# Graph attention on one core: the softmax sums in quarters of columns spread over a group, two accumulators for GpSimd, the residuals in other groups, the MLP weights cast in eight parts

## Chip, cores and metric

One core of a Trainium2 chip. The metric is the device time of one execution in microseconds (us); less is better. Engines: PE (TensorE), DVE (VectorE), ACT (ScalarE), POOL (GpSimd) and SP (SyncE, which here issues most DMAs). PE's weight loads have a row of their own in the profile, PEld.

## What is computed

A layer of graph attention over 2048 nodes with D = 256, 8 heads of 32 and a hidden width of 1024, all in float32:

```
h   = relu(layernorm(x))
hs  = layer_norm(h) * ln1_scale + ln1_bias          (sources)
ht  = layer_norm(h_target) * ln1_scale + ln1_bias   (targets)
q, k, v = ht @ Wq + bq, hs @ Wk + bk, hs @ Wv + bv  (q divided by sqrt(32))
probs = softmax(where(adj != 0, q k^T, -1e30))      (per head, 2048 x 2048)
y   = layer_norm(ht + (probs v) @ Wo + bo) * ln2_scale + ln2_bias
out = x + y + gelu(y @ W1) @ W2
```

The softmax takes no maximum: exponentials are used as they are, their sums are kept, and the context is divided by the sums later. (A slower path for very large values follows at the end and does not run on these inputs.)

## The kernel before

It is written by hand: each engine has its own program, and semaphores tie them together, so the order on an engine is the order of its code.

**Stages.** Layer norms, transposes and the projections of keys, values and queries come first (to about 66 us). Then the attention (to about 375 us), then the output products, the second layer norm and the MLP for four chunks of 512 targets.

**The attention loop** has 128 tiles. The targets are cut into 4 chunks `c` of 512 columns, the heads into 2 groups `g` of 4, the sources into 16 tiles `i` of 128. A tile is k = 32c + 16g + i, and G = 2c + g (0 to 7) counts the groups of 16 tiles. A tile holds two pairs of heads, u = 2k and 2k + 1, each a block of 128 x 1024 in a ring `probs` of 12 pairs, so 6 tiles. Per tile:

- PE, `scores` (L1387 to L1408): three times four products (high and low parts of keys and queries) of 512 columns into PSUM `slot` (three of them for pairs). It waits until DVE has emptied what the slots held.
- DVE, `mask` (L1017 to L1033): for each pair one instruction takes the minimum of scores and mask into `probs`.
- ACT, `exponentials` (L750): one exponential for each pair, in place.
- PE, `weigh` (L1410 to L1427): values times probabilities, four products of 512 columns side by side into `acc[:, 0]`. It waits for both exponentials of the tile.
- The sums of the probabilities over the 16 tiles. For the tiles in `ADDED` (L50) POOL adds them up into `added_up` (`add_up`, L535), two instructions per tile. For those in `TAKEN` PE multiplies them with ones into `acc[:, 1]` (`sum_weights`, L1429), one half of 256 columns in the tile's own iteration and one in the next. `close` (L1445) multiplies POOL's total with ones at i = 1 of the next group, and ACT copies the sums out (`evacuate_sums`, behind exponential u = 5 of the next group).

A float32 product is two passes on PE, so the profile counts four products as x8. PE runs two tiles ahead with the scores:

```
for k in range(NT):
    if k + 2 < NT:
        scores(k + 2)
    if k == NT - 2:
        attend(0)
    weigh(k)
    if k and (k - 1) % ST in TAKEN:
        sum_weights(k - 1, 1)
    if k % ST in TAKEN:
        sum_weights(k, 0)
    if k % ST == 1 and k > ST:
        close(k // ST - 1)
```

DVE masks a pair only when the ring's pair from six tiles back is done with: it waits for PE (`used`) and, for tiles in `ADDED`, for POOL (`added`).

**Around the loop.** At each chunk's end SP stores the sums, loads them packed, DVE inverts them (`invert`, at u % 64 = 14 of the next chunk, L1014), SP stores and spreads the inverses (`spread_inverse`, L387), and POOL multiplies the context with them (`divide`). In the last chunk SP issues the DMAs of W1 and W2 (L450, L451) just behind `spread_inverse(2)`; they go into the space of a mask that is no longer used (`w1_raw`, `w2_raw`, views of `maskT`). ACT casts W1 whole behind exponential 220 and W2 whole behind exponential 238 (`split_weights`, L768). POOL takes the difference w1_lo (L588) between the last chunk's two groups, DVE w2_lo (L1137) behind the loop. POOL also prepares the residual in `htn` (`make_residual`, L557), two instructions for each chunk.

**Behind the loop** PE does `attend(2)`, `turn_y(0)` (transposes, after DVE's layer norm of chunk 0), `attend(1)` and the first MLP products (`widen`). ACT loads the gelu table behind the last copy of the sums.

Of the kernel before, what the change touches and what calls it, by code (L numbers as in the profile page):

```python
# [32 lines left out]
def graph_attention(nc, x, adj, nodemask, h_target, ln1_scale, ln1_bias, Wq, bq, Wk, bk, Wv, bv, Wo, bo,  # L33
# [16 lines left out]
    ADDED = [0, 1, 3, 5, 7, 9, 11, 13]  # L50
    TAKEN = [i for i in range(ST) if i not in ADDED]
    OPS = (len(ADDED) - 1) * PAIRS

# [22 lines left out]
    with ExitStack() as ctx:  # L76
# [156 lines left out]
        ht_kept = sem("ht_kept")  # L233
        q_kept = sem("q_kept")
# [15 lines left out]
        used = sem("used")  # L250
# [80 lines left out]

        def packed(saved, c):
            return saved[:, cols_of(c)].rearrange("h (a b) -> h a b", b=PACK)
# [25 lines left out]
        SLOW_MIX = 8 + 3 * NEWTON + 5  # L359
        UG = PAIRS * ST  # L360
# [3 lines left out]
        def _(sp):  # L364
# [72 lines left out]
            for c in range(NCH):  # L437
# [22 lines left out]
            sp.wait_ge(used, NT)  # L460
# [50 lines left out]
        def _(pool):  # L511
# [23 lines left out]
            def add_up(c, g, i, pair):  # L535
                k = (c * GROUPS + g) * ST + i

                def at(tile):
                    return probs[:, ((k - i + tile) * PAIRS + pair) % RING]
                pool.wait_ge(exped, k * PAIRS + pair + 1)  # L540
                if i == ADDED[1]:
                    if k >= ST:
                        pool.wait_ge(closed, c * GROUPS + g)
                    nc.gpsimd.tensor_tensor(added_up[:, pair], at(ADDED[0]), at(i), ALU.add).then_inc(added, 1)  # L544
                else:
                    pool.wait_ge(added, added_through(k, pair) - PAIRS)
                    nc.gpsimd.tensor_tensor(added_up[:, pair], added_up[:, pair], at(i), ALU.add).then_inc(added, 1)  # L547
# [9 lines left out]
            def make_residual(c, step):  # L557
                h = htn[:, rows_of(c), :]
                if step == 0:
                    if c == 0:  # L560
                        pool.wait_ge(rest_made, 2)
                        pool.wait_ge(ht_kept, 16)
                    nc.gpsimd.tensor_tensor(h, h, gamma1_row[:, None, :].to_broadcast(wide), ALU.mult
# [6 lines left out]
            for c in range(NCH):  # L570
                for g in range(GROUPS):
                    for i in ADDED[1:]:
# [9 lines left out]
                    if c < LAST:  # L582
                        make_residual(c, g)
                    elif g == 0:
                        divide(c - 1, 0)
                        divide(c - 1, 1)
                        pool.wait_ge(w1_hi_made, 1)
                        nc.gpsimd.tensor_tensor(w1_lo[:], w1_raw, w1_hi[:].bitcast(F32), ALU.subtract  # L588
                                                ).then_inc(w1_lo_made, 1)
# [16 lines left out]
        def _(act):  # L606
# [161 lines left out]
            def split_weights(step):  # L768
                if step == 0:
# [3 lines left out]
                    nc.scalar.copy(w1_hi[:], w1_raw).then_inc(w1_hi_made, 1)  # L773
                else:
# [888 lines left out]
```

## Time and profile before

| | |
|---|---|
| median of three runs | 495.03 us (492.99, 495.03, 495.15) |
| profiled execution | 494.16 us, span 492.5 us |
| busy PE / DVE / ACT / POOL | 473.9 / 419.1 / 377.1 / 305.4 us |
| mean granted TensorE clock | 0.995 of full speed |
| DMA traffic | 46.92 MB, mean 95 GB/s |

The span runs from the first to the last instruction. Rows below are from this one execution. In a timeline, instructions of a kind that follow one another are merged into a row: start, length of the whole run, engine, line, operation, output and inputs, count, and, in brackets, the idle time just before it with what ended it. PE's products overlap one another in such rows, so PE's pace is read from starts. A clock of 1.00 is 2.4 GHz, 0.50 is 1.2 GHz.

### The profile page before, as it was taken

The numbers are of one execution on the slowest core, as the hardware profiler recorded it, in microseconds if no ns is written. First come the engines' busy times: TensorE is split into PE (matmuls) and PEld (weight loads), VectorE is DVE, ScalarE is ACT, GpSimd is POOL, SyncE is SP. The second block draws the span as 40 slices with busy tenths as digits, with TensorE's granted clock in tenths as the row PEclk, the third lists the DMA queues.
The fourth block names the chain that finished last, engine by engine and source line by source line (L and its number), as shares of the span: only waits on it lengthen the run. The fifth ranks groups of instructions, "written<-read, shape, count | busy, mean of one in ns | idle before, by whom it ended". The sixth has DMA issues, their size and how long they took to land.

```text
span 492.5 us, 10622 instructions
## 1 busy us (share of the span) xinstructions
PE 473.9 (96%) x4366; PEld 244.3 (50%) x4366; DVE 419.1 (85%) x631; ACT 377.1 (77%) x456; POOL 305.4 (62%) x152
## 2 busy tenths in 40 slices
PE   3999979999999999999999999999999999999995
PEld 1567523433333333333333333343434888888884
DVE  6889479999999999999999999999997977666343
ACT  4987968998998898998898998999995570727150
POOL 1000019996998999999999998999998300000000
PEclk9999989999999999999999999999999999999999
DMA  8997789723543674222772400070000100202021
GB/s 232 266 219 124 186 249 402 236 44 63 200 74 44 67 171 79 44 46 46 82 179 50 83 2 3 12 207 1 2 2 1 46 28 17 87 1 85 1 85 45
DMA packets 53774, 46.92 MB, mean 95 GB/s; under 512 B 35486, under 2 KB 46652, under 8 KB 53212
## 3 DMA queue, kind: packets, MB, share of 16 engines
q1 hardware_dynamic: 51216, 37.30, 28.3%
q0 software_dynamic: 2480, 8.92, 10.7%
q8 instruction: 35, 0.57, 0.5%
q14 instruction: 15, 0.12, 0.1%
q10 hardware_dynamic: 28, 0.01, 0.0%
HBM read 31.93 MB, written 14.81 MB: 95 GB/s over the span
## 4 chain that ended last, share of the span: by engine, by line
PE 61%; DVE 14%; issue 13%; ACT 5%; POOL 5%; DMA 1%; DVEq 0%; POOLq 0%
PE acc L1421 14%; PE slot L1406 13%; DVE probs L1032 10%; PE acc L1439 6%; PE slot L1521 3%; PE slot L1520 3%; PE slot L1519 3%; POOL added_up L547 3%; PE acc L1557 2%; PE acc L1558 2%; PE acc L1556 2%; PE slot L1472 2%; PE slot L1308 2%; DVE stats L852 1%; PE slot L1328 1%
## 5 line engine op out<-in xcount | busy, mean ns | idle before, releaser
L1032 DVE SCALAR_TENSOR_TENSOR probs<-maskT,slot 128x1024 f32<-128x1024 uint16 x256 | 298.4, 1217 | 8.1 <-PE slot L1406 7.8
L753 ACT ACTIVATE probs<-probs 128x1024 f32<-128x1024 f32 x256 | 267.0, 1057 | 25.7 <-DVE probs L1032 7.2
L547 POOL TENSOR_TENSOR added_up<-added_up,probs 128x1024 f32<-128x1024 f32 x96 | 226.7, 2417 | 1.0 <-ACT probs L753 0.9
L1421 PE MATMUL acc<-probs,V 128*32 128x512 f32 x1024 | 137.1, 607 | 1.0 <-ACT probs L753 1.0
L1439 PE MATMUL acc<-probs,ones 128*32 128x256 f32 x1024 | 77.1, 379 | 0.0
L1439 PEld LDWEIGHTS acc<-probs,ones 128*32 128x32 f32 x1024 | 33.3, 110 | 72.8 <-issue 71.2
L1406 PE MATMUL slot<-q_hi,k_hi 32*128 32x512 f32 x512 | 64.8, 496 | 3.8 <-DVE probs L1032 3.5
L544 POOL TENSOR_TENSOR added_up<-probs 128x1024 f32<-128x1024 f32 x16 | 38.1, 2411 | 29.4 <-ACT probs L753 18.8
L1406 PEld LDWEIGHTS slot<-q_hi,k_hi 32*128 32x128 f32 x512 | 24.6, 182 | 61.9 <-DVE probs L1032 55.2
L810 ACT ACTIVATE g_full<-slot 128x512 f32<-128x512 f32 x32 | 19.3, 602 | 45.2 <-issue 30.0
L1406 PE MATMUL slot<-q_lo,k_hi 32*128 32x512 f32 x512 | 52.0, 392 | 0.0
L1406 PE MATMUL slot<-q_hi,k_lo 32*128 32x512 f32 x512 | 51.8, 392 | 0.0
L1421 PEld LDWEIGHTS acc<-probs,V 128*32 128x32 f32 x1024 | 20.3, 108 | 48.3 <-issue 43.0
L516 POOL DMA_DIRECT2D adj_raw<-in_adj x16 | 8.9, 557 | 47.2 <-DMA maskT<-adj_raw 36.3
L1087 DVE TENSOR_TENSOR g_lo<-g_full,g_hi 128x512 fp32r<-128x512 f32 x32 | 23.0, 718 | 17.2 <-ACT g_hi L811 17.1
L1406 PEld LDWEIGHTS slot<-q_lo,k_hi 32*128 32x128 f32 x512 | 25.0, 184 | 4.8
L1519 PE MATMUL slot<-yT_hi,w_hi 128*128 128x512 f32 x64 | 25.6, 399 | 0.0
L1406 PEld LDWEIGHTS slot<-q_hi,k_lo 32*128 32x128 f32 x512 | 25.1, 185 | 0.0
L1521 PE MATMUL slot<-yT_hi,w_lo 128*128 128x512 f32 x64 | 25.0, 390 | 0.0
L1520 PE MATMUL slot<-yT_lo,w_hi 128*128 128x512 f32 x64 | 24.9, 389 | 0.0
L811 ACT ACTIVATE g_hi<-slot 128x512 fp32r<-128x512 f32 x32 | 19.1, 597 | 0.0
L1556 PE MATMUL acc<-g_hi,w_hi 128*128 128x512 f32 x48 | 18.9, 394 | 0.0
(142 smaller groups left out, 496.7 us busy)
## 6 DMA issues: line engine op xcount, KB each, us to landing
adj_raw<-in_adj POOLq DMA_DIRECT2D x16, 512.0 KB, 5.4
htn<-in_L_gnn_h_target SPq DMA_DIRECT2D x4, 512.0 KB, 5.7
ht_saved<-htn SPq DMA_DIRECT2D x1, 2048.0 KB, 6.8
k_hi_saved<-k_hi SPq DMA_DIRECT2D x1, 2048.0 KB, 10.6
k_lo_saved<-k_lo SPq DMA_DIRECT2D x1, 2048.0 KB, 14.1
v_saved<-V SPq DMA_DIRECT2D x1, 2048.0 KB, 9.0
inverse<-inverse_saved SPq DMA_DIRECT2D x8, 256.0 KB
maskT<-in_L_gnn_W SPq DMA_DIRECT2D x2, 1024.0 KB, 12.3
```

Of the source, the lines that this page charges most:

```text
L544: nc.gpsimd.tensor_tensor(added_up[:, pair], at(ADDED[0]), at(i), ALU.add).then_inc(added, 1)
L547: nc.gpsimd.tensor_tensor(added_up[:, pair], added_up[:, pair], at(i), ALU.add).then_inc(added, 1)
L753: nc.scalar.activation(p, p, ACT.Exp).then_inc(exped, 1)
L1032: nc.vector.scalar_tensor_tensor(out=probs[:, u % RING], in0=m, scalar=-HALF_EDGE, in1=slot[u % SLOTS][:], op0=ALU.add, op1=ALU.min).then_ ...
L1087: nc.vector.tensor_tensor(g_lo[:, f, :], g_full[:, f % 2, :], g_hi[:, f, :].bitcast(F32), ALU.subtract).then_inc(gelu_lo, 1)
L1406: mm = pe.matmul(slot[(PAIRS * k + j // 2) % SLOTS][:, j % 2, :], keys_part[head, g, i * P:(i + 1) * P], queries_part[head, g, :], start=( ...
L1421: mm = pe.matmul(acc[HD * j:HD * j + HD, 0, :], V[:, i, h * HD:(h + 1) * HD], probs[:, (PAIRS * k + j // 2) % RING, j % 2, :], start=(i == 0),
L1439: mm = pe.matmul(acc[HD * j:HD * j + HD, 1, ts], ones[:], probs[:, (PAIRS * k + j // 2) % RING, j % 2, ts], start=first and not half, stop ...
L1519: pe.matmul(dst, w1_hi[:, d, fs], yT_hi[:, d, :], start=(d == 0), stop=False)
L1520: pe.matmul(dst, w1_hi[:, d, fs], yT_lo[:, d, :], start=False, stop=False)
L1521: mm = pe.matmul(dst, w1_lo[:, d, fs], yT_hi[:, d, :], start=False, stop=(d == DC - 1))
L1556: pe.matmul(dst, w2_hi[:, f, ds], g_hi[:, f, :], start=(f == 0), stop=False)
```

## The change

It has five parts.

1. **PE's sums.** Each group's nine units of sums (eight tiles in `TAKEN` and POOL's total) are 36 quarters of 128 columns. `QUARTERS` gives each of the 16 iterations 2 or 3 of them, beginning at i = 3 of the group and ending at i = 2 of the next with POOL's total. Adjoining quarters of one tile are one product, of 128, 256 or 384 columns. `close` and the semaphore `used` are gone. The sums' copy on ACT moves to u = 7 of the next group. After the loop, the quarters of the last tile that PE sums come at once, those of POOL's total behind `attend(2, [0, 1, 2])`.
2. **POOL's adds.** `ADDED` is 0, 1, 2, 4, 7, 9, 11, 13 instead of 0, 1, 3, 5, 7, 9, 11, 13. Even groups add into the second half of `htn` (`added_spare`), odd ones into `added_up`. SP reloads that half of `htn` in the last chunk.
3. **Residuals.** Those of chunk 1 go into groups 2 and 5, those of chunk 2 behind all adds; w1_lo goes between the adds of the last group.
4. **Casts.** W1 and W2 are cast in four parts each, of 512 columns, behind exponentials 212, 217, 222, 227 (W1) and 232, 237, 242, 247 (W2).
5. **Gelu table.** It is loaded before the last copy of the sums.

```diff
-    ADDED = [0, 1, 3, 5, 7, 9, 11, 13]
+    ADDED = [0, 1, 2, 4, 7, 9, 11, 13]
+    QUARTERS = [2, 2, 3, 2] * (ST // 4)
+    FIRST = 3
+    QUARTER = CHUNK // 4
...
+        SPARE = slice(2 * TILES, 4 * TILES)
+        added_spare = htn[:, SPARE, :].rearrange("p t d -> p (t d)").rearrange(
+            "p (a b n) -> p a b n", a=PAIRS, b=2)
+        def added_at(G):
+            return added_up if G % 2 else added_spare
...
+        SPLITS = 4
+        SPLIT_EVERY = 5
+        SPLIT_FROM = PAIRS * (NT - ST) - 12
...
+                if c == LAST:
+                    sp.wait_ge(ht_kept, 16)
+                    sp.dma_start(htn[:, SPARE, :], ht_saved[:, SPARE, :]).then_inc(ht_again, 16)
...
-            sp.wait_ge(used, NT)
+            sp.wait_ge(closed, NCH * GROUPS)
...
+                total = added_at(G)[:, pair]
                 if i == ADDED[1]:
-                    if k >= ST:
-                        pool.wait_ge(closed, c * GROUPS + g)
-                    nc.gpsimd.tensor_tensor(added_up[:, pair], at(ADDED[0]), at(i), ALU.add).then_inc(added, 1)
+                    if G == 0:
+                        pool.wait_ge(ht_kept, 16)
+                    elif G >= 2:
+                        pool.wait_ge(closed, G - 1)
+                    nc.gpsimd.tensor_tensor(total, at(ADDED[0]), at(i), ALU.add).then_inc(added, 1)
...
+                        if c == LAST and g == 1 and i == ADDED[3]:
+                            pool.wait_ge(w1_hi_made, SPLITS)
+                            nc.gpsimd.tensor_tensor(w1_lo[:], w1_raw, w1_hi[:].bitcast(F32), ALU.subtract
+                                                    ).then_inc(w1_lo_made, 1)
...
             def split_weights(step):
                 if step == 0:
                     act.wait_ge(w1_in, 16)
                     act.wait_ge(scored, GT * LAST)
                     act.wait_ge(q_kept, 32 * NCH)
-                    nc.scalar.copy(w1_hi[:], w1_raw).then_inc(w1_hi_made, 1)
-                else:
+                elif step == SPLITS:
                     act.wait_ge(w2_in, 16)
-                    nc.scalar.copy(w2_hi[:], w2_raw).then_inc(w2_hi_made, 1)
+                if step < SPLITS:
+                    d, fs = step // 2, slice(step % 2 * FF // 2, (step % 2 + 1) * FF // 2)
+                    nc.scalar.copy(w1_hi[:, d, fs], w1_raw[:, d, fs]).then_inc(w1_hi_made, 1)
...
-                if u % UG == 5 and u > 5:
+                if u % UG == 7 and u > 7:
                     evacuate_sums(u // UG - 1)
-                if u in (PAIRS * NT - 36, PAIRS * NT - 18):
-                    split_weights(int(u == PAIRS * NT - 18))
+                if u >= SPLIT_FROM and (u - SPLIT_FROM) % SPLIT_EVERY == 0:
+                    split_weights((u - SPLIT_FROM) // SPLIT_EVERY)
...
-                if k and (k - 1) % ST in TAKEN:
-                    sum_weights(k - 1, 1)
-                if k % ST in TAKEN:
-                    sum_weights(k, 0)
-                if k % ST == 1 and k > ST:
-                    close(k // ST - 1)
-            sum_weights(NT - 1, 1)
-            close(NCH * GROUPS - 1)
+                G = k // ST - (k % ST < FIRST)
+                if G >= 0:
+                    sum_weights(G, k % ST)
+            for at in range(FIRST):
+                sum_weights(NCH * GROUPS - 1, at, range(len(TAKEN)))
...
             attend(2, [0, 1, 2])
+            for at in range(FIRST):
+                sum_weights(NCH * GROUPS - 1, at, [len(TAKEN)])
             turn_y(0)
```

How the order on the engines changes is shown at three places. First PE, around the end of the first group: weighing is `acc<-probs,V`, a sum is `acc<-probs,ones`, POOL's total `acc<-added_up,ones`, and counts are products. Before, from iteration 15 to iteration 17:

```order
L1421 MATMUL acc<-probs,V 32x512 x4
L1439 MATMUL acc<-probs,ones 32x256 x8
L1406 MATMUL slot<-q_hi,k_hi 128x512 x4
L1406 MATMUL slot<-q_hi,k_lo 128x512 x4
L1406 MATMUL slot<-q_lo,k_hi 128x512 x4
L1421 MATMUL acc<-probs,V 32x512 x4
L1439 MATMUL acc<-probs,ones 32x256 x4
L1406 MATMUL slot<-q_hi,k_hi 128x512 x4
L1406 MATMUL slot<-q_hi,k_lo 128x512 x4
L1406 MATMUL slot<-q_lo,k_hi 128x512 x4
L1421 MATMUL acc<-probs,V 32x512 x4
L1448 MATMUL acc<-added_up,ones 32x512 x4
```

With the change, from iteration 14 to iteration 16:

```order
L1460 MATMUL acc<-probs,V 32x512 x4
L1481 MATMUL acc<-probs,ones 32x384 x4
L1445 MATMUL slot<-q_hi,k_hi 128x512 x4
L1445 MATMUL slot<-q_hi,k_lo 128x512 x4
L1445 MATMUL slot<-q_lo,k_hi 128x512 x4
L1460 MATMUL acc<-probs,V 32x512 x4
L1481 MATMUL acc<-probs,ones 32x128 x8
L1445 MATMUL slot<-q_hi,k_hi 128x512 x4
L1445 MATMUL slot<-q_hi,k_lo 128x512 x4
L1445 MATMUL slot<-q_lo,k_hi 128x512 x4
L1460 MATMUL acc<-probs,V 32x512 x4
L1481 MATMUL acc<-probs,ones 32x256 x4
```

The iterations with eight products of 256 columns and with the closing products of 512 are gone; instead some have 384 columns, and some have two pieces of 128.

Second ACT, from the sums' copy of group 5 into the last group: `probs<-probs` are exponentials, `w_hi<-maskT` the casts. Before:

```order
L766 ACTIVATE sums_wide<-acc 128x512
L753 ACTIVATE probs<-probs 128x1024 x23
L773 CAST w_hi<-maskT 128x2048
L753 ACTIVATE probs<-probs 128x1024 x5
L760 COPY context<-acc 128x512
L753 ACTIVATE probs<-probs 128x1024 x4
L766 ACTIVATE sums_wide<-acc 128x512
L753 ACTIVATE probs<-probs 128x1024 x9
L776 CAST w_hi<-maskT 128x2048
L753 ACTIVATE probs<-probs 128x1024 x17
```

With the change:

```order
L800 ACTIVATE sums_wide<-acc 128x512
L787 ACTIVATE probs<-probs 128x1024 x13
L812 CAST w_hi<-maskT 128x512
L787 ACTIVATE probs<-probs 128x1024 x5
L812 CAST w_hi<-maskT 128x512
L787 ACTIVATE probs<-probs 128x1024 x5
L812 CAST w_hi<-maskT 128x512
L787 ACTIVATE probs<-probs 128x1024 x3
L794 COPY context<-acc 128x512
L787 ACTIVATE probs<-probs 128x1024 x2
L812 CAST w_hi<-maskT 128x512
L787 ACTIVATE probs<-probs 128x1024 x4
```

The first cast now stands 13 exponentials behind the sums' copy, which itself is two exponentials later, instead of 23; each cast has a quarter of the columns.

Third POOL, from the end of group 5 on: `added_up` and `htn<-probs` are adds, `w_lo` is w1_lo. Before:

```order
L553 TENSOR_TENSOR context<-context,inverse 128x512
L567 TENSOR_TENSOR htn<-htn,rest_row 128x1024
L544 TENSOR_TENSOR added_up<-probs 128x1024 x2
L547 TENSOR_TENSOR added_up<-added_up,probs 128x1024 x12
L553 TENSOR_TENSOR context<-context,inverse 128x512 x2
L588 TENSOR_TENSOR w_lo<-maskT,w_hi 128x2048
L544 TENSOR_TENSOR added_up<-probs 128x1024 x2
L547 TENSOR_TENSOR added_up<-added_up,probs 128x1024 x12
```

With the change:

```order
L569 TENSOR_TENSOR htn<-probs 128x1024 x2
L572 TENSOR_TENSOR htn<-htn,probs 128x1024 x12
L578 TENSOR_TENSOR context<-context,inverse 128x512 x2
L569 TENSOR_TENSOR added_up<-probs 128x1024 x2
L572 TENSOR_TENSOR added_up<-added_up,probs 128x1024 x4
L609 TENSOR_TENSOR w_lo<-maskT,w_hi 128x2048
L572 TENSOR_TENSOR added_up<-added_up,probs 128x1024 x8
L590 TENSOR_TENSOR htn<-htn,gamma_row 128x1024
L594 TENSOR_TENSOR htn<-htn,rest_row 128x1024
L590 TENSOR_TENSOR htn<-htn,gamma_row 128x1024
L594 TENSOR_TENSOR htn<-htn,rest_row 128x1024
```

w1_lo moved from before the last group's adds to behind six of them, and the two instructions for the residual of chunk 2 now follow the adds.

## Rows read from the trace of the kernel before

**Rows 1.** The page's costliest groups: busy, mean ns, idle before, releaser.
```profile
L1032 DVE SCALAR_TENSOR_TENSOR probs<-maskT,slot 128x1024 f32<-128x1024 uint16 x256 | 298.4, 1217 | 8.1 <-PE slot L1406 7.8
```

**Rows 2.** Timeline of PE, 107 to 112: start us, us, engine, line, operation.
```profile
107.12 0.51 PE L1406 MATMUL slot<-q_hi,k_hi 32*128 32x512 f32 x4
...
108.91 1.05 PE L1439 MATMUL acc<-probs,ones 128*32 128x256 f32 x16
109.88 0.50 PE L1406 MATMUL slot<-q_hi,k_hi 32*128 32x512 f32 x4
...
110.78 1.06 PE L1421 MATMUL acc<-probs,V 128*32 128x512 f32 x8
...
112.21 0.50 PE L1406 MATMUL slot<-q_hi,k_hi 32*128 32x512 f32 x4
```

**Rows 3.** Timeline of DVE, 104 to 145.
```profile
110.91 1.22 DVE L1032 SCALAR_TENSOR_TENSOR probs<-maskT,slot 128x1024 f32<-128x1024 uint16 x1 [0.41 <-PE slot L1406]
...
144.12 4.65 DVE L1032 SCALAR_TENSOR_TENSOR probs<-maskT,slot 128x1024 f32<-128x1024 uint16 x4 [0.15 <-PE slot L1406]
```

**Rows 4.** Timeline of ACT, 320 to 340.
```profile
319.05 13.88 ACT L753 ACTIVATE probs<-probs 128x1024 f32<-128x1024 f32 x12
332.83 1.89 ACT L773 CAST w_hi<-maskT 128x2048 fp32r<-128x2048 f32 x1
```

**Rows 5.** Timeline of PE, 325 to 338.
```profile
325.83 1.06 PE L1421 MATMUL acc<-probs,V 128*32 128x512 f32 x8
...
334.25 0.51 PE L1406 MATMUL slot<-q_hi,k_hi 32*128 32x512 f32 x4
...
337.16 0.50 PE L1406 MATMUL slot<-q_hi,k_hi 32*128 32x512 f32 x4
```

**Rows 6.** Timeline of DVE, 315 to 361.
```profile
315.33 0.35 DVE L1014 RECIPROCAL inverses<-sums 128x32 f32<-128x32 f32 x1
...
360.59 2.35 DVE L1032 SCALAR_TENSOR_TENSOR probs<-maskT,slot 128x1024 f32<-128x1024 uint16 x2 [0.55 <-PE slot L1406]
```

**Rows 7.** SP's timeline, and the landing of what writes maskT from 318 to 319.2.
```profile
318.75 0.48 SPq L450 DMA_DIRECT2D maskT<-in_L_gnn_W  x1
...
DMA to landing us min/median/max: 11.2/11.2/11.2
```

**Rows 8.** Timeline of PE, 381 to 390.
```profile
381.63 2.86 PE L1472 MATMUL slot<-wo,context 128*128 128x256 f32 x12
384.33 1.04 PE L1502 MATMUL slot<-ident,htn 128*128 128x128 f32 x8
...
389.33 0.58 PE L1519 MATMUL slot<-yT_hi,w_hi 128*128 128x512 f32 x1
```

**Rows 9.** Timeline of DVE at 383.
```profile
382.80 1.38 DVE L1076 TENSOR_SCALAR htn<-htn,second,rstd 128x256 f32<-128x256 f32 x4
```

**Rows 10.** Timeline of POOL, 341 to 380.
```profile
341.80 4.70 POOL L588 TENSOR_TENSOR w_lo<-maskT,w_hi 128x2048 fp32r<-128x2048 f32 x1
...
351.05 28.32 POOL L547 TENSOR_TENSOR added_up<-added_up,probs 128x1024 f32<-128x1024 f32 x12
```

**Rows 11.** DMA issues of the whole span: KB each, median us to landing.
```profile
maskT<-in_L_gnn_W SPq DMA_DIRECT2D x2, 1024.0 KB, 12.3
...
q_hi<-q_hi_saved SPq DMA_DIRECT2D x2, 512.0 KB, 7.3
```

**Rows 12.** Windows: length; busy PE, PEld, DVE, ACT, POOL; granted clock; DMA share; GB/s.
```profile
67.00:71.00 4.00, 1.01 (x16) 0.56 (x12) 3.97 (x4) 3.28 (x3) 0.00 (x0) 0.99 0.71 139
71.00:74.00 3.00, 2.78 (x20) 1.04 (x20) 2.37 (x3) 2.12 (x3) 1.66 (x1) 0.50 1.01 379
74.00:75.00 1.00, 1.00 (x12) 0.43 (x12) 1.00 (x2) 0.81 (x1) 1.00 (x2) 0.83 1.01 375
```

**Rows 13.** Timeline of PE, 71 to 75.
```profile
71.22 0.80 PE L1406 MATMUL slot<-q_hi,k_hi 32*128 32x512 f32 x4 [1.32 <-DVE probs L1032]
...
74.53 0.51 PE L1406 MATMUL slot<-q_hi,k_hi 32*128 32x512 f32 x4
```

More of the change, by code:

```diff
@@ L811, in gelu @@
                     nc.scalar.activation(g_hi[:, f, :], h, ACT.Gelu_apprx_tanh).then_inc(gelu_hi, 1)
-            nc.scalar.activation(warm[:], columns[:, 0:1], ACT.Gelu_apprx_tanh).then_inc(warmed, 1)
             y_affine(0)
@@ L1425, in weigh, with sum_part, sum_weights @@
                     mm.then_inc(context_done, 1)
-                elif i in ADDED:
-                    mm.then_inc(used, 1)
-            def sum_weights(k, half):
-                c, g, i = place(k)
-                G = c * GROUPS + g
-                ts = slice(half * CHUNK // 2, (half + 1) * CHUNK // 2)
-                first = i == TAKEN[0]
-                if first and G and not half:
+            def sum_part(G, n, low, high):
+                ts = slice(low * QUARTER, high * QUARTER)
+                last = n == len(TAKEN)
+                if last and low == 0:
+                    pe.wait_ge(added, OPS * (G + 1))
+                if n == 0 and low == 0 and G:
                     pe.wait_ge(sums_out, G)
                 for j in range(PER):
-                    mm = pe.matmul(acc[HD * j:HD * j + HD, 1, ts], ones[:],
-                                   probs[:, (PAIRS * k + j // 2) % RING, j % 2, ts],
-                                   start=first and not half, stop=False)
-                if half:
-                    mm.then_inc(used, 1)
-            def close(G):
-                pe.wait_ge(added, OPS * (G + 1))
-                for j in range(PER):
-                    mm = pe.matmul(acc[HD * j:HD * j + HD, 1, :], ones[:], added_up[:, j // 2, j % 2, :],
-                                   start=False, stop=True)
-                mm.then_inc(closed, 1)
+                    if last:
+                        weights = added_at(G)[:, j // 2, j % 2, ts]
+                    else:
+                        weights = probs[:, (PAIRS * (G * ST + TAKEN[n]) + j // 2) % RING, j % 2, ts]
+                    mm = pe.matmul(acc[HD * j:HD * j + HD, 1, ts], ones[:], weights,
+                                   start=(n == 0 and low == 0), stop=last and high == 4)
+                if last and high == 4:
+                    mm.then_inc(closed, 1)
+            def sum_weights(G, at, tiles=range(len(TAKEN) + 1)):
+                visit = (at - FIRST) % ST
+                begin = sum(QUARTERS[(FIRST + v) % ST] for v in range(visit))
+                end = begin + QUARTERS[at]
+                for n in tiles:
+                    low, high = max(begin - 4 * n, 0), min(end - 4 * n, 4)
+                    if low < high:
+                        sum_part(G, n, low, high)
             def attend(c, tiles=range(TILES)):
```

30 lines of the change are left out of this document (20 added, 10 removed).

## The prediction

> **What bounds the kernel now.** I read the page's costliest groups first. Half of the instructions belong to one loop over 128 tiles (tile k = 16G + i, group G = 0 to 7), and the vector engine's masking is busy for 298.4 us of it and idle for 8.1 us, nearly all of it for scores from the tensor engine (PE) [rows 1]. So DVE looks like the limit. The timeline of PE says otherwise. The scores of two successive tiles start 2.33 us apart (109.88 to 112.21), and nothing on PE is missing in between: scores 0.90 us, then 1.43 us for weighing and one half of a tile's sums, which is six passes of 256 columns at 0.216 and 0.13 of changeover. Where a visit has two halves (108.91, x16) the next scores start 2.76 us after the last ones [rows 2]. A second half costs 0.43 us, and DVE idles 0.41 us just behind it [rows 3] without the loop ever making it up. **PE's own work sets the pace; DVE merely has almost as much.** Whatever the change does to the number of columns PE sums counts in full; how they are spread does not.
>
> Three other things reach the path. The cast of W1 on ACT, 1.89 us [rows 4], holds exponentials back, and scores start 2.91 us apart instead of 2.33 (334.25 to 337.16) [rows 5]: 0.58 us; the cast of W2 shows as 0.55 us of idle DVE [rows 6]. The DMAs that bring W1 and W2 are issued late: W1 at 318.75 us, and it lands 11.2 us later, at 329.95 [rows 7]. Behind the loop, PE goes from the product of chunk 2 (381.63) over the transposes (384.33, just behind the normalised rows, 382.80 + 1.38 on DVE) to the first MLP product at 389.33 [rows 8, 9].
>
> **Sums in quarters.** Up to tile 125 (the output product for chunk 0 follows at iteration 126, and the end hangs on it) the old loop has 14 double visits: i = 15 in seven groups and i = 1 (the closing product) seven times; 14 x 0.43 = 6.0 us above the base of two quarters. The new one has visits of three quarters at i = 2, 6, 10, 14, 30 of them up to there, at half of 0.43, so 30 x 0.216 = 6.5. Net **+0.4 us**: visit 2 of the first group, which used to sum, now has nothing to do, and that time is not used. So the even spread gains nothing by itself. One side effect does: DVE has pauses of its own, 0.15 us at the start of three chunks [rows 3] and about 0.1 us at each of the three reciprocals (0.35 us, mostly absorbed [rows 6]). They delay the scores of i = 1 and i = 9, which is just where a third quarter now delays PE anyway. Both no longer add up: **-0.7 us** (bounds 0 and -0.75).
>
> Pieces of 128 columns: eight of them per group, replacing four of 256. No row shows such a product in four column tiles. The transposes of 128 columns start (1.04 - 0.27)/7 = 0.110 us apart, with 0.27 for the last one [rows 8]: half of 0.216 plus 0.002. Each product is two passes, so 128 passes cost 0.3 us; I take **+0.2**. Bounds: 0, and 1.2 us if each lost 9 ns, which is by how much the twelve products of 256 columns at 381.63, (2.86 - 0.38)/11 = 0.225 us apart [rows 8], stand above 0.216. I take the transposes, whose width is the same.
>
> **Pool.** It adds twelve times in 28.32 us [rows 10], 2.36 each, so 33 us for a group's fourteen, of some 38.1 us. With two accumulators it need not wait for the closing product. Nobody but Pool waits there now, so this is **0**. What hides Pool is the ring of six tiles. In the last group the adds of tile 7 come behind the adds of tiles 1, 2 and 4 and the 4.70 us of w1_lo: started 4.7 us after the group's first mask, 4.7 + 6 x 2.36 + 4.7 + 2 x 2.36 = 28.3, and wanted by the mask of tile 13, at 13 x 2.38 = 31. If that cover went, each late add would hold a mask. The residual of chunk 2 moves behind the last add. Tile 113's scores start at 337.16 [rows 5], mask and exponential are done some 3.3 us later (1.03, 1.22 and 1.06 [rows 2 to 4]), then 33 + 4.7 + 2 x 2.4 ends at 383. DVE asks for it after the normalised rows (384.2 [rows 9]) and w2_lo. The reload of half of htn on SP's queue goes behind the weights' DMAs and lands long before.
>
> **ACT.** Both stalls of the casts go: **-1.15 us**, since a part of 512 columns is a quarter of 1.89, about 0.5 us, and ACT has more than that to spare in each tile (two exponentials of 1.06 in 2.33, overlapping a little). The sums' copy moves by a tile, as does the closing product: 0.
>
> **But the first part is asked for too early.** The old cast stood behind exponential 220; the first part stands behind exponential 212, eight earlier. Twelve exponentials, 209 to 220, start at 319.05 [rows 4], (13.88 - 1.06)/11 = 1.165 us apart, so 212, the fourth, starts at 322.5 and ends at 323.6. W1 lands at 329.95 [rows 7]. That DMA is not issued earlier than before: it is on SP's queue behind the inverses, which wait for a reciprocal that DVE makes at mask 206 (315.33) [rows 6], and both move together with the loop. So ACT stands for 6.3 us with exponential 213 queued behind the wait. It then copies (0.5), takes exponential 213 (1.06) and releases the weighing of tile 106 at about 331.6. In the trace that began at 325.83 [rows 5]. **+5.8 us**, and a loop bound by PE does not recover it. Bounds: the page has the two weight DMAs at a median of 12.3 us [rows 11], which makes it 6.9; a DMA of half the size lands in 7.3 [rows 11], which makes it 1.9. I take 11.2, the same DMA behind the same neighbours.
>
> **The clock.** In that wait PE is idle for nearly 6 us. The trace has one comparable place: from 67 to 71 us PE was busy for 1.01 us, then the granted clock was 0.50 (1.2 GHz) from 70.96 on and back at full speed (2.4 GHz) at 74.3, some 3.4 us [rows 12]. Scores started 3.31 us apart there (71.22 to 74.53) [rows 13] instead of 2.33, so 1.0 us was lost; all of it under work would be 1.7, and two such stretches 3.4. I take **+1.6**. The Trainium skill speaks against the change here too: "TensorE: Matmul & The Clock Gate", in "HAM oscillation — how this bites in real kernels", describes waits in the stream of products that bring the lower clock back and reckons the loss as throttled time x (1 - 1.2/2.4). By that rule, on the 3.4 us of this trace, the sum below would be 500.6; if the clock did not fall it would be 498.9.
>
> **The tail.** Before the product of chunk 2 PE has five quarters less, behind it the four quarters of the closing product, while it would otherwise wait for the normalised rows: three tiles of that product end at about 383.4, the quarters at 384.2, and with two changeovers of 0.1 the transposes slip from 384.33 by **+0.2 us**. Loading the gelu table before the sums' copy keeps ACT off that path: 0.
>
> **Sum.** The profiled execution took 494.16 us (span 492.5 and 1.7 around it); the median of the three runs shown is 495.03, 0.9 above it. 494.16 + 0.4 - 0.7 + 0.2 - 1.15 + 0.2 = 493.1 without the wait for W1; + 5.8 + 1.6 = **500.5 us**.
>
> **Rivals.** (1) *W1 is there in time.* If the DMA landed within 5 us of its issue, ACT would not wait, and the kernel takes 493.1: not slower. It decides at 323.6 us. For it: nothing but the DMA engines' load makes it 11.2 us. Against: even the 7.3 us of half the size [rows 11] would end at 326.1, and the queue's order stays. 7%. (2) *PE has slack, and the spread works.* If a single extra quarter fitted into each tile, DVE's 14 pauses of 0.41 us would go, 5.7 us: 500.5 - 5.7 = 494.8, not slower, and 487.4 if (1) held too. It decides on whether scores behind a visit of three quarters start 2.33 or 2.54 us apart. For it: DVE's rate of 1.165 us per mask looks like a limit. Against: the double visit is passed on at 0.43 us in full, so there is nothing left to fit into. 8%, and 2% of it with (1). (3) *The wait holds, but the clock stays up:* 498.9. Or it stays low for two stretches, or the small pieces are dear: 502 to 504. These are inside the forecast's case.
>
> **How the numbers follow.** The forecast's case, a wait of several us, has 85%. Faster by over 0.5% needs both rivals or more gain than I can find: 0.04. Within 0.5% of 495.03 (492.6 to 497.5; about what a measurement can tell from no change): 0.13. Slower: 0.83. The range leaves out the 1 in 10 near 494 and the dearest ends: 496.3 (a wait shortened to about 3 us) to 503.3 (the late landing, and the clock down for longer).
>
> **What would show it.** Right: ACT idle for about 6 us before its first cast of 512, released by the DMA of W1; PE without work for nearly 6 us around 326 to 332, and a granted clock of half behind it; scores 2.54 us apart behind three quarters and 2.33 elsewhere; no stall at the later parts; Pool's wait for the closing product gone with no effect. Wrong: a first cast that starts within 1 us of its exponential; tiles at 2.33 throughout; DVE or the final residual waiting for Pool.

## The result, and the profile after

| | before | after | ratio, 95% interval |
|---|---|---|---|
| median of 5 runs, us | 495.03 (492.99 to 495.15) | 505.4 (503.49 to 506.17) | 1.0211 (1.018 to 1.0243) |
| profiled execution, us | 494.16, span 492.5 | 506.16, span 504.5 | |

The kernel became 10.4 us slower. The prediction said 500.5 us, slower, and at most 503.3. The profiled executions lie 12.0 us apart, and these are the 12.0 us that are laid out here; before, the profiled execution lies 0.9 us below the median, after, 0.8 above it.

The page of after has more idle time on the vector engine (DVE) for scores, and GpSimd (POOL) still adds fourteen times a group, now into two tensors:

```profile
L1071 DVE SCALAR_TENSOR_TENSOR probs<-maskT,slot 128x1024 f32<-128x1024 uint16 x256 | 298.7, 1217 | 15.1 <-PE slot L1445 14.4
...
L572 POOL TENSOR_TENSOR htn<-htn,probs 128x1024 f32<-128x1024 f32 x48 | 113.5, 2393 | 9.7 <-ACT probs L787 9.6
L572 POOL TENSOR_TENSOR added_up<-added_up,probs 128x1024 f32<-128x1024 f32 x48 | 113.4, 2400 | 0.1
```

A mask costs what it did [rows 1] and waits 7 us longer. POOL now waits for exponentials and no longer for the closing product. So I cut both executions at the same events, which are starts of instructions in the timelines. In us:

| from, to | before | after | difference |
|---|---|---|---|
| start, scores of tile 5 | 79.16 | 79.86 | +0.70 |
| tile 5, tile 108 | 245.78 | 245.34 | -0.44 |
| tile 108, tile 110 | 4.66 | 12.83 | +8.17 |
| tile 110, tile 127 | 41.62 | 40.49 | -1.13 |
| tile 127, first residual add on DVE | 6.09 | 6.10 | 0 |
| that add, w2_lo on DVE (the layer norm between) | 6.79 | 9.70 | +2.91 |
| w2_lo, first MLP product | 5.24 | 6.81 | +1.57 |
| first MLP product, end | 103.15 | 103.34 | +0.19 |

**The largest piece is the wait for W1.** ACT's timeline of after, 316 to 338 us (start, us, engine, line, operation):

```profile
320.50 3.40 ACT L787 ACTIVATE probs<-probs 128x1024 f32<-128x1024 f32 x3 [0.22 <-DVE probs L1071]
330.42 0.62 ACT L812 CAST w_hi<-maskT 128x512 fp32r<-128x512 f32 x1 [6.53 <-DMA maskT<-in_L_gnn_W]
```

The chain of waits has the whole transfer in it (start, us, what):

```profile
318.94 11.46 DMA maskT<-in_L_gnn_W
332.05 1.94 PE acc L1460 x8
```

The timeline of the tensor engine (PE), 324 to 345 us:

```profile
325.21 0.51 PE L1445 MATMUL slot<-q_hi,k_hi 32*128 32x512 f32 x4
...
332.05 1.94 PE L1460 MATMUL acc<-probs,V 128*32 128x512 f32 x8 [5.86 <-ACT probs L787]
...
335.19 0.80 PE L1445 MATMUL slot<-q_hi,k_hi 32*128 32x512 f32 x4
...
338.04 0.50 PE L1445 MATMUL slot<-q_hi,k_hi 32*128 32x512 f32 x4
...
340.37 0.51 PE L1445 MATMUL slot<-q_hi,k_hi 32*128 32x512 f32 x4
...
342.71 0.50 PE L1445 MATMUL slot<-q_hi,k_hi 32*128 32x512 f32 x4
```

W1 was issued at 318.94 and landed 11.46 us later. ACT stood idle for 6.53 us with exponentials queued behind the cast, and PE for 5.86. Then weighing took 1.94 us instead of the 1.06 of [rows 5], and the scores of tiles 109 and 110 are 2.85 us apart (335.19, 338.04) before 2.33 comes back. The windows say why (length; busy PE, PEld, DVE, ACT, POOL; granted clock; DMA share; GB/s):

```profile
326.00:328.00 2.00, 0.19 (x4) 0.00 (x0) 2.00 (x3) 0.00 (x0) 0.38 (x1) 1.00 1.09 230
328.00:330.00 2.00, 0.00 (x0) 0.00 (x0) 0.59 (x1) 0.00 (x0) 0.00 (x0) 0.89 0.80 268
330.00:332.00 2.00, 0.00 (x0) 0.00 (x0) 0.00 (x0) 1.58 (x3) 0.00 (x0) 0.50 0.31 103
332.00:334.00 2.00, 1.95 (x16) 0.63 (x20) 0.00 (x0) 2.00 (x3) 0.98 (x1) 0.50 0.08 26
334.00:336.00 2.00, 2.00 (x24) 1.09 (x20) 0.00 (x0) 2.00 (x3) 2.00 (x2) 0.50 0.00 0
336.00:338.00 2.00, 2.00 (x24) 0.54 (x20) 1.26 (x2) 0.30 (x2) 1.73 (x1) 0.91 0.00 0
```

The granted clock fell to 0.50 (1.2 GHz) while PE was still idle, and was back (2.4 GHz) only 4.3 us after it had work again: it was low from 329.55 to 336.38 (the 0.89 and 0.91 above are windows that it shares with full speed), and PE worked from 332.05 on.

**The second piece was not in the prediction.** The timeline of after behind the loop, 384 to 395 us, DVE, POOL and PE together:

```profile
386.39 2.37 POOL L590 TENSOR_TENSOR htn<-htn,gamma_row 128x1024 f32<-128x1024 f32 x1
...
387.75 1.04 DVE L1094 TENSOR_SCALAR spread<-second 128x4 f32<-128x4 f32 x1
...
388.82 0.17 DVE L1096 TENSOR_SCALAR rstd<-spread 128x4 int32<-128x4 int32 x1
388.83 2.36 POOL L594 TENSOR_TENSOR htn<-htn,rest_row 128x1024 f32<-128x1024 f32 x1
389.02 2.20 DVE L1099 TENSOR_SCALAR rstd<-rstd 128x4 int32<-128x4 int32 x1
390.90 1.07 PE L1481 MATMUL acc<-added_up,ones 128*32 128x128 f32 x16
391.26 0.16 DVE L1103 TENSOR_TENSOR newton<-rstd 128x4 f32<-128x4 f32 x1
```

Two instructions on 128x4 elements, which take 0.17 us elsewhere, took 1.04 and 2.20. Each ends with an instruction of POOL: 387.75 + 1.04 = 388.79 beside 386.39 + 2.37 = 388.76, and 391.22 beside 391.19. These are the two operations of chunk 2's residual, which the change put behind the loop. The 2.90 us that they add are the 2.91 us of the table. The transposes wait for the rows that are normalised there, so PE pauses, and the clock fell once more. PE's timeline and the windows at that place:

```profile
394.47 1.97 PE L1543 MATMUL slot<-ident,htn 128*128 128x128 f32 x8 [2.50 <-DVE htn L1115]
```

```profile
392.00:394.00 2.00, 0.00 (x0) 0.00 (x0) 1.79 (x9) 0.60 (x1) 0.00 (x0) 1.00 0.01 4
394.00:396.00 2.00, 1.53 (x7) 1.54 (x8) 2.00 (x3) 0.00 (x0) 0.00 (x0) 0.60 0.03 5
396.00:398.00 2.00, 2.00 (x8) 1.70 (x7) 0.61 (x1) 1.52 (x3) 0.00 (x0) 0.55 0.69 203
```

The transposes took 1.97 us instead of 1.04 [rows 8], and the four products behind them 1.81 instead of 1.03. Together they are the +1.57, but for 0.1 us by which the transposes start closer to w2_lo.

The +0.70 at the start lies before anything that the change touches. The half clock that both kernels have there [rows 12] lasted till 77 us in this execution:

```profile
71.00:74.00 3.00, 2.86 (x20) 1.04 (x20) 2.37 (x4) 2.12 (x2) 1.74 (x1) 0.50 1.07 300
74.00:77.00 3.00, 3.00 (x21) 1.04 (x20) 1.91 (x3) 2.12 (x2) 3.00 (x3) 0.51 1.01 382
```

The kernels below that are built from after have the same code up to there. In their profiled executions small_residual had the long stretch too and came to tile 5 at 80.03 us; loads_early, casts_later and both_mended had one of 3.4 us (79.13 to 79.33), and residual_held_back had none (78.11). So it belongs to the execution and not to the change.

### The profile page after: what moved, and what is told of

Read it like the earlier page. It is cut to its first block, busy times and chain, and to the rows that moved or that the text cites. A ratio compares the mean times of both kernels' runs of the same rounds, so it can differ in the third digit from the quotient of the medians.

```text
span 504.5 us, 11021 instructions
## 1 busy us (share of the span) xinstructions
PE 478.8 (95%) x4622; PEld 253.1 (50%) x4622; DVE 422.0 (84%) x631; ACT 377.5 (75%) x462; POOL 305.8 (61%) x152
## 3 DMA queue, kind: packets, MB, share of 16 engines
q0 software_dynamic: 2480, 8.92, 10.6%
## 4 chain that ended last, share of the span: by engine, by line
PE 83%; DVE 8%; ACT 4%; DMA 3%; issue 1%; DVEq 0%
PE acc L1460 23%; PE slot L1445 22%; PE acc L1481 11%; PE slot L1562 3%; PE slot L1560 3%; PE slot L1561 3%; DMA maskT<-in_L_gnn_W 2%; DVE probs L1071 2%; PE acc L1597 2%; PE acc L1599 2%; PE acc L1598 2%; PE slot L1347 2%; PE slot L1516 2%; DVE stats L891 2%; PE slot L1367 1%
## 5 line engine op out<-in xcount | busy, mean ns | idle before, releaser
L1071 DVE SCALAR_TENSOR_TENSOR probs<-maskT,slot 128x1024 f32<-128x1024 uint16 x256 | 298.7, 1217 | 15.1 <-PE slot L1445 14.4
L572 POOL TENSOR_TENSOR htn<-htn,probs 128x1024 f32<-128x1024 f32 x48 | 113.5, 2393 | 9.7 <-ACT probs L787 9.6
L572 POOL TENSOR_TENSOR added_up<-added_up,probs 128x1024 f32<-128x1024 f32 x48 | 113.4, 2400 | 0.1
L1481 PE MATMUL acc<-probs,ones 128*32 128x256 f32 (+2 forms) x1216 | 77.7, 348 | 0.0
L1481 PEld LDWEIGHTS acc<-probs,ones 128*32 128x32 f32 x1216 | 38.8, 111 | 72.9 <-issue 71.3
L569 POOL TENSOR_TENSOR htn<-probs 128x1024 f32<-128x1024 f32 x8 | 18.9, 2387 | 21.0 <-ACT probs L787 21.0
L569 POOL TENSOR_TENSOR added_up<-probs 128x1024 f32<-128x1024 f32 x8 | 19.0, 2396 | 5.6 <-ACT probs L787 5.6
```

The costliest lines, as they stand in the source:

```text
L569: nc.gpsimd.tensor_tensor(total, at(ADDED[0]), at(i), ALU.add).then_inc(added, 1)
L572: nc.gpsimd.tensor_tensor(total, total, at(i), ALU.add).then_inc(added, 1)
L1071: nc.vector.scalar_tensor_tensor(out=probs[:, u % RING], in0=m, scalar=-HALF_EDGE, in1=slot[u % SLOTS][:], op0=ALU.add, op1=ALU.min).then_ ...
L1481: mm = pe.matmul(acc[HD * j:HD * j + HD, 1, ts], ones[:], weights, start=(n == 0 and low == 0), stop=last and high == 4)
```

## The experiments

**1. loads_early.** The two weight DMAs of after stand ahead of the sums and inverses in SP's queue:

```diff
+                if c == LAST:
+                    sp.wait_ge(masked, UC * c)
+                    sp.dma_start(w1_raw, W1.rearrange("(c p) n -> p c n", p=P)).then_inc(w1_in, 16)
+                    sp.dma_start(w2_raw, W2.rearrange("(f p) n -> p f n", p=P)).then_inc(w2_in, 16)
...
-                if c == LAST:
-                    sp.wait_ge(masked, UC * c)
-                    sp.dma_start(w1_raw, W1.rearrange("(c p) n -> p c n", p=P)).then_inc(w1_in, 16)
-                    sp.dma_start(w2_raw, W2.rearrange("(f p) n -> p f n", p=P)).then_inc(w2_in, 16)
```

> The changed kernel with one edit: SP issues the DMAs of W1 and W2 as soon as the last mask of chunk 2 is made (mask 192), ahead of the sums and the inverses. Theory A (ACT's first cast stood 7 us for the DMA of W1, and the clock fell behind that): scores of tiles 108 to 110 are 4.7 us apart instead of 12.8, no idle ACT before the first cast, about 8 us less, 497 us. What then remains above the kernel before is in the tail. Rival (the wait sits on top of something else, so that ACT or the ring would stop there anyway): less than 3 us gained, above 502.

Measured: 497.74 us (495.45 to 498.59), ratio to before 1.0063 (1.0044 to 1.0083), span 493.8. ACT's timeline has the cast right behind its exponentials:

```profile
319.78 3.39 ACT L787 ACTIVATE probs<-probs 128x1024 f32<-128x1024 f32 x3 [0.22 <-DVE probs L1071]
323.07 0.60 ACT L812 CAST w_hi<-maskT 128x512 fp32r<-128x512 f32 x1
323.58 5.37 ACT L787 ACTIVATE probs<-probs 128x1024 f32<-128x1024 f32 x5
```

W1 is issued at 296.96 us and lands at 302.25, 5.3 us later instead of 11.5: in after the two transfers of the inverses, 256 KB each, stand in the queue 0.6 and 1.2 us ahead of it, here they do not (the likely reason, not tested by itself). So the late place cost twice, by the issue and by a landing time that was twice as long. Tile 108 to 110 takes 4.87 us instead of 12.83. The wait and its clock cost 7.96 us; the 0.21 that is left over before is a visit of three quarters. The layer norm still takes 9.73 us, with POOL over the same two instructions:

```profile
377.69 2.38 POOL L590 TENSOR_TENSOR htn<-htn,gamma_row 128x1024 f32<-128x1024 f32 x1
...
379.03 1.07 DVE L1094 TENSOR_SCALAR spread<-second 128x4 f32<-128x4 f32 x1
...
380.15 2.36 POOL L594 TENSOR_TENSOR htn<-htn,rest_row 128x1024 f32<-128x1024 f32 x1
380.34 2.20 DVE L1099 TENSOR_SCALAR rstd<-rstd 128x4 int32<-128x4 int32 x1
```

The profiled execution is the fastest of the four (495.45 us, mean granted clock 0.994). The others took 497.22 to 498.59 at 0.987 to 0.992, so the clock fell for longer there; where, no profile shows.

**2. casts_later.** The other end of the same wait: the DMAs stay, the casts start at exponential 220.

```diff
-        SPLIT_FROM = PAIRS * (NT - ST) - 12
+        SPLIT_FROM = PAIRS * (NT - ST) - 4
```

> The changed kernel with the first cast behind exponential 220 instead of 212 (the others follow every five), the DMAs as they are. Theory A: the DMA of W1 has landed when ACT asks, so the same gain as with early DMAs, about 8 us, 497 us. If instead the late DMAs themselves disturb the loop, only the kernel with early DMAs gains and this one stays above 502.

Measured: 496.31 us in a single run, span 494.6, tile 108 to 110 in 4.87 us. ACT's timeline has no wait for W1 any more:

```profile
332.80 0.60 ACT L812 CAST w_hi<-maskT 128x512 fp32r<-128x512 f32 x1
```

The distance between issue and cast is what counts; either end mends it. The second loss is here too, and a little larger: with POOL 0.5 us later beside DVE than in loads_early, L1094 takes 1.58 us and L1099 2.21, and the layer norm 10.24. PE pauses for 3.04 us before the transposes, but the clock stays at 1.00 there.

**3. small_residual.** After, with chunk 2's residual on one column for each tile of nodes.

```diff
-            make_residual(2, 0)
-            make_residual(2, 1)
+            pool.wait_ge(ht_again, 16)
+            for step in range(2):
+                h = htn[:, rows_of(2), 0:1]
...
+                nc.gpsimd.tensor_tensor(h, h, gamma1_row[:, None, 0:1].to_broadcast([P, TILES, 1]), ALU.mult
```

> The changed kernel, but POOL's two instructions for the residual of chunk 2 take 4 columns instead of 1024 (that residual is left out, otherwise as before). Theory B (while POOL runs those two of 2.4 us behind the loop, DVE's small instructions of the layer norm stand until POOL is done, 2.9 us in sum; PE then pauses, and its clock falls, 1.6 us): L1094 and L1099 take 0.17 us each, no PE pause before the transposes, no second stretch at half clock; 4.5 us less, 501 us. Rival (the gelu table's load on ACT, which now runs at the same moment, holds DVE): nothing changes, 505.

Measured: 501.16 us (500.3 to 501.92), ratio 1.0121 (1.0102 to 1.0139), span 500.2. The timeline, 384 to 390 us:

```profile
386.61 0.48 POOL L626 TENSOR_TENSOR htn<-htn,gamma_row 128x4 f32<-128x4 f32 x2
...
387.93 0.17 DVE L1098 TENSOR_SCALAR spread<-second 128x4 f32<-128x4 f32 x1
387.95 1.28 ACT L831 ACT_TABLE_LOAD   x1
...
388.34 0.17 DVE L1103 TENSOR_SCALAR rstd<-rstd 128x4 int32<-128x4 int32 x1
```

The layer norm is back at 6.79 us, both instructions at 0.17, and ACT's table load, which also lies there, does nothing to them. The clock does not fall at the transposes either; w2_lo to the MLP is 5.54 us.

**4. both_mended.** Experiments 1 and 3 together.

> Early DMAs and the small residual together (the residual of chunk 2 left out). If A and B are all there is, the gains add up: 505.4 - 8.2 - 4.5 = 492.7 us, 1 to 2 us below the kernel before, which is what the casts (1.15) and the coincidence of DVE's pauses with the third quarters (0.4) are worth. If quarters and small pieces cost something of their own, it stays above 495.

Measured: 494.15 us (493.25 to 494.69), ratio 0.9987 (0.9977 to 0.9997), span 491.6. Nothing of the loss is left. The expected 492.7 was not reached: against the runs of before that were made beside it (median 494.85) the kernel gains 0.7 us, and 0.9 in the profiled span, where 1 to 2 were expected. By stages that is 1.15 us won in tile 110 to 127 and 0.42 in the loop, less 0.21 at tile 108 and 0.3 in the tail. And it is a kernel that leaves most of one residual out.

**5. casts_alone.** Before, with the early DMAs and the casts in eight parts, and nothing else of the change.

```diff
-                if u in (PAIRS * NT - 36, PAIRS * NT - 18):
-                    split_weights(int(u == PAIRS * NT - 18))
+                if u in (216, 218, 220, 222, 232, 237, 242, 247):
+                    split_weights((216, 218, 220, 222, 232, 237, 242, 247).index(u))
```

> The kernel before, with only the casts of W1 and W2 in eight parts (behind exponentials 216, 218, 220, 222, then 232, 237, 242, 247) and the DMAs of W1 and W2 issued early so that they are there. My step on the casts says the two stalls of 0.58 and 0.57 us go: 1.15 us less, about 493.7. If the parts still stop PE somewhere, less is gained, and the scores' spacing shows where.

Measured: 493.98 us (492.77 to 494.37), ratio 0.9977 (0.9966 to 0.9988), span 491.2. The loop up to tile 108 takes 245.75 us, as before, and tile 110 to 127 40.54, against 41.62 before and 40.47 to 40.49 with the whole change. All that the change gains in its last group comes from the casts. Four of them come two exponentials apart here, and ACT needs 2.41 us for two exponentials and a part (328.29 to 330.71), slightly more than a tile's 2.33; PE does not feel four in a row, the scores stay 2.33 us apart. This is the fastest complete kernel of the study.

**6. quarters_alone.** Before, with PE's sums in quarters and nothing else: one accumulator, residuals and casts as they were.

> The kernel before, with only PE's sums in quarters (one accumulator, the old tiles, residuals and casts in the old places). My steps say: loop 0.3 to 0.5 us less (third quarters fall on DVE's own pauses), tail 0.2 more, so no change within 0.5%: 494.5. The rival that the spread itself works (DVE's pauses of 0.41 us go) says 489.

Measured: 499.76 us (499.2 to 499.9), ratio 1.0095 (1.0074 to 1.0115), span 498.2. A miss by 5 us. Of these, 1.3 lie at the start (tile 5 at 80.43; already tile 0 is at 67.25 instead of 66.07), ahead of all that the edit touches. The loop to tile 108 takes 248.53 us, 2.75 more than before, and tile 110 to 127 42.72. The waits of this kernel (us in total, times, longest) have a line which neither before nor after has:

```profile
DVE probs L1053 <- POOL added_up L564: 3.2, 6, 0.5
```

So six masks wait for POOL's adds, 0.53 us each, and PE does not get it back. In the last group it is more: the mask of tile 119 starts 2.20 us behind its scores, and the next scores come 3.47 us behind the last ones, which is about the 1.1 us of that stretch. DVE's timeline, third group:

```profile
162.31 2.35 DVE L1053 SCALAR_TENSOR_TENSOR probs<-maskT,slot 128x1024 f32<-128x1024 uint16 x2 [0.53 <-POOL added_up L564]
```

**7. quarters_tiles.** The same with the change's set of tiles for POOL, to tell the set from the accumulator.

```diff
-    ADDED = [0, 1, 3, 5, 7, 9, 11, 13]
+    ADDED = [0, 1, 2, 4, 7, 9, 11, 13]
```

> The kernel of quarters_alone (TensorE's sums in quarters, one accumulator on GpSimd) with the change's set of tiles that GpSimd adds (0, 1, 2, 4, 7, ... in place of 0, 1, 3, 5, 7, ...). In the trace of quarters_alone the scores of tiles 8 start 2.85 us behind those of tiles 7 in every group, because the mask of tile 7 starts 1.58 us behind its scores instead of 1.02 (DVE probs <- POOL added_up). Theory: the single accumulator is to blame. In quarters the closing product of a group comes later, GpSimd may not open the next group before it, and is then half a microsecond late with an old tile whose slot the mask of tile 7 wants. By this theory the other set of tiles makes it worse or no better: tile 2 has to be added where tile 3 had to, so the mask that reuses its slot comes one tile earlier (tile 6), and GpSimd is late by some 2 to 2.5 us more at that point; the stretch from the scores of tile 5 to those of tile 108 takes 248.5 us or more, up to 2 us in each of six groups more (260), and the time is 500 to 512. Rival: the set of tiles, not the accumulator, is what quarters_alone lacked; then the stretch falls to the 245.4 us of loads_early and the time to 496.5.

Measured: 499.05 us (497.6 to 499.32), ratio 1.0087 (1.007 to 1.0104), span 495.9. The loop takes 248.49 us, the same as in 6, so the set is not to blame. That the accumulator is, POOL's row below shows: it had been idle for 2.12 us when the closing product let it open the group. My extra, a worse wait one tile earlier, did not come: it is still the mask of tile 7 that waits. The ring holds six tiles, so this mask reuses the slot of tile 1, which POOL's first two adds read, and those open the accumulator. POOL's timeline of this kernel, and then of loads_early, third group:

```profile
155.20 4.76 POOL L564 TENSOR_TENSOR added_up<-probs 128x1024 f32<-128x1024 f32 x2 [2.12 <-PE acc L1463]
```

```profile
149.53 4.76 POOL L569 TENSOR_TENSOR htn<-probs 128x1024 f32<-128x1024 f32 x2 [1.66 <-ACT probs L787]
```

The group's first scores start at 142.87 and 143.33. So POOL opens 12.3 us behind them with one accumulator, after the closing product in quarters, and 6.2 with two. In casts_alone, with halves and one accumulator, it is 153.62 - 143.05 = 10.6 us, and DVE does not wait there.

**8. residual_held_back.** loads_early, with chunk 2's residual at full size but kept until the rows are normalised.

```diff
+            pool.wait_ge(norm_y, LN2)
             make_residual(2, 0)
```

> Early DMAs as in loads_early, and POOL's two instructions for the residual of chunk 2 wait for DVE's layer norm of chunk 0 to end. Theory B in its narrow form (a DVE instruction stands while a POOL instruction runs, and the other way round): the layer norm takes 6.8 us again instead of 9.7, but now POOL and w2_lo meet: the second to start stands for the first, add_residual(2) comes 2.4 to 4.8 us later than in both_mended, 497 to 499 us, no better than loads_early. If POOL merely were late in general, the layer norm would stay at 9.7.

Measured: 499.15 us (498.33 to 499.37), ratio 1.0088 (1.0068 to 1.0108), span 496.7. The layer norm is at 6.80 us with the same work on POOL, only later. But the loss moved on, and grew: w2_lo to the MLP takes 9.51 us, 4.3 more than in loads_early, and from there to the end it is 105.47 instead of 102.93, since the granted clock is 0.50 from 389.64 to 396.47. The timeline, 380 to 392 us:

```profile
381.68 2.29 DVE L1177 TENSOR_TENSOR w_lo<-maskT,w_hi 128x2048 fp32r<-128x2048 f32 x1
381.85 4.34 POOL L590 TENSOR_TENSOR htn<-htn,gamma_row 128x1024 f32<-128x1024 f32 x1 [5.12 <-DVE htn L1116]
...
388.71 1.22 DVE L1085 TENSOR_TENSOR htn<-slot,htn 128x1024 f32<-128x1024 f32 x1 [4.74 <-POOL htn L594]
...
391.19 0.80 PE L1561 MATMUL slot<-yT_hi,w_hi 128*128 128x512 f32 x1 [3.62 <-DVE yT_lo L1122]
```

Here DVE was first, by 0.17 us, and POOL paid: 4.34 us for an operation of 2.37. Then DVE's add of chunk 2 waits for the residual, and PE waits for DVE.

**9. all_mended.** Early DMAs, casts from exponential 204, quarters, the spare accumulator in groups 1, 3 and 5 only, chunk 2's residual and w1_lo between the last two groups.

```diff
-            return added_up if G % 2 else added_spare
+            return added_spare if G in (1, 3, 5) else added_up
...
+                        make_residual(2, 0)
+                        make_residual(2, 1)
```

> A kernel with the change's quarters and parts and nothing left out: early DMAs, casts from exponential 204 on, the spare accumulator for groups 1, 3 and 5 only, so that half of htn is reloaded in group 6 and the residual of chunk 2 and w1_lo run on POOL between the last two groups. If A and B are the whole loss, it is as fast as both_mended: 494 us, 0 to 1 us below the kernel before. If the last group's adds come too late (POOL starts 7 us into it), DVE shows waits for POOL and it is 495 to 497.

Measured: 495.18 us (494.45 to 496.43), ratio 1.0007 (0.9996 to 1.0018), span 493.0. Loop 245.36 and layer norm 6.80 us as hoped, but tile 110 to 127 takes 42.00 instead of 40.47. POOL starts the last group late, behind the residual (337.87 to 342.75) and w1_lo. POOL's timeline, 60 to 400 us, and DVE's, 348 to 362:

```profile
342.70 4.63 POOL L615 TENSOR_TENSOR w_lo<-maskT,w_hi 128x2048 fp32r<-128x2048 f32 x1
347.26 4.77 POOL L569 TENSOR_TENSOR added_up<-probs 128x1024 f32<-128x1024 f32 x2
```

```profile
349.79 1.22 DVE L1070 SCALAR_TENSOR_TENSOR probs<-maskT,slot 128x1024 f32<-128x1024 uint16 x1 [0.17 <-POOL added_up L569]
352.14 9.53 DVE L1070 SCALAR_TENSOR_TENSOR probs<-maskT,slot 128x1024 f32<-128x1024 uint16 x8 [1.12 <-PE slot L1444]
```

The second pause of DVE is put down to PE's scores, but the mask starts 2.2 us behind them instead of 1.0, and at 352.14, just behind the end of POOL's two opening adds (352.03), which read its slot. So POOL has no free 4.8 us before the last group. Not all of the 1.5 us are the residual's, for the last two groups share one accumulator here: that alone lets POOL open only 12.3 us behind a group's first scores, and costs 0.5 us a group (experiment 7). Here POOL opens 13.1 us behind them. About 1 us is left for the residual, an estimate from these numbers; no run has it in that place with two accumulators.

## Why the prediction was right and wrong

By its own steps, against the profiled executions:

- **Loop in quarters, +0.4 and DVE's pauses, -0.7**: -0.3 predicted. Measured are -0.44 up to tile 108, and +0.21 for one more visit of three quarters behind it. The net is right; no run takes its two terms apart. So is the pace: 340.37 to 342.71 is 2.34 us, and tiles behind three quarters follow at 2.54.
- **Small pieces, +0.2**: not seen on their own; the +0.21 at tile 108 is the third quarter, and what the pieces cost is inside the -0.44. Neither confirmed nor refuted.
- **The casts' stalls, -1.15**: -1.13 measured, and shown to be the casts by casts_alone. The reason given was a little off: ACT does not have more to spare in each tile than a part takes (2.41 us against 2.33).
- **The wait for W1, +5.8, and the clock, +1.6**: 7.4 predicted, 7.96 measured. PE idled 5.86 us, so the wait was right to 0.1, and some 2.1 are left for the clock. I had sized it from a stretch of 3.4 us [rows 12]; here it was 6.8 us, 4.3 of them under work, and at half the clock half of that is lost: 2.2.
- **The tail, +0.2**: in small_residual, where nothing holds the layer norm, it is 5.54 - 5.24 = 0.3. In after itself PE waited for DVE there in any case.
- **Pool: "The residual of chunk 2 moves behind the last add."** This is the step that failed. I asked only when its result is wanted, put its end at 383 and had DVE ask for it later. It ended at 391.2, and that it was late for no one is true; but what it does to DVE *while it runs* I had at nothing. It costs 2.91 us, and by the pause that it makes on PE another 1.57, of which the prediction had 0.2, as its tail. small_residual and residual_held_back show the first: less work at that time, or the same work at another time, and the loss is gone from that place. The second was gone in small_residual; in the profiled executions of loads_early and casts_later it was gone with the residual in place (5.20 us in both), so it is a risk of that pause rather than a sure cost.
- **"With two accumulators ... this is 0"**: right against the kernel before, but for a thin reason. With halves POOL is in time with one accumulator; with quarters it is not, and the second one saves the 3.1 us of the loop that quarters_tiles loses against loads_early (248.49 and 245.36).

The sum for the profiled run: 500.5 + 0.7 for the start + 0.6 for the wait + 2.9 for the layer norm + 1.4 for what follows it is 506.1, against 506.16. (The prediction started its sum from the profiled 494.16; from the median of 495.03 it would have been 501.4, inside its range all the same.) The rival that W1 is there in time and the rival that PE has slack both fell; the one that "stays low for two stretches" was nearest for the clock and too small for the rest. The range ended at 503.3 because no case in it had a price for DVE and POOL side by side. Its list of signs could not have warned either: every sign of "right" came, and "DVE waiting for Pool" does not show as a wait. The waits of after have no line of DVE for POOL; a held instruction only looks long.

The trace of before had that price. Its timeline, 391 to 394 us:

```profile
391.46 2.40 POOL L567 TENSOR_TENSOR htn<-htn,rest_row 128x1024 f32<-128x1024 f32 x1
...
392.83 1.57 DVE L1087 TENSOR_TENSOR g_lo<-g_full,g_hi 128x512 fp32r<-128x512 f32 x1
```

The same g_lo takes 0.69 us elsewhere (0.71 in the mean of after's page); here it ends 0.54 us behind POOL's.

The Trainium skill has the rule in "SBUF — State Buffer", "Who interferes with whom": DVE and GpSimd share one pair of ports as an exclusive lock held for a whole instruction; tensor_scalar can take it, in the modes that use both of DVE's port pairs; tensor_tensor with both inputs in SBUF conflicts with a GpSimd instruction that reads SBUF; a DVE instruction with at most one SBUF input outside those modes does not; and whichever starts first makes the other wait. By that rule the trace agrees: the tensor_scalar rows are held to POOL's end, POOL's to DVE's in experiment 8, and the masks of the loop, whose scores come from PSUM, keep their 1217 ns beside POOL's adds. What the runs show themselves is that the held instructions end with the other engine's; in which mode DVE ran them no trace tells.

## What to carry to other kernels

Work that moves to an idle engine can still hold a busy one there, as POOL's residual held DVE's layer norm for 2.9 us: look for a place in the old trace where the two run side by side, and compare the durations there with the usual ones. Before a consumer is moved forward, subtract the issue time of its DMA and the landing time from its new place; here eight exponentials of 1.165 us turned a hidden load of 11.5 us into a wait of 6.5. And take the landing time from the place where the DMA will stand: the same transfer took 11.5 us behind two others and 5.3 without them. Last, take the parts of a change one by one: of this one only the casts gained (-1.1 us), the quarters needed the second accumulator to cost nothing, and the second accumulator was what pushed the residual behind the loop.

## What the hardware showed beyond that

- How long the clock stays down is not the same each time. A pause of 5.86 us on PE gave 6.8 us at half clock, one of 3.62 (residual_held_back) again some 6.8, one of 2.50 (after) 3.4, and at the same place one of 2.53 in loads_early and one of 3.04 in casts_later gave none.
- How small the held instruction is does not matter: 128x4 elements waited up to 2 us. Who starts first does: at 388.82 in after a DVE instruction of 0.17 us began 0.01 us ahead of POOL's second and took its usual time, and the next, at 389.02, was held until POOL's ended.
